# Second layer: a ring of eight activation buffers, second products held back ahead of the decays, decays a turn ahead, softplus without a mask

## What is computed

```
dt = softplus(u @ W_dt.T + b_dt)                     # u: layer-normed x, per token and channel
state = exp(dt * A[:, n]) * state + dt * B[:, n] * u # n = 0..15, along 512 tokens
y = sum_n C[:, n] * state_n + D * u
probs = softmax(u @ router_w + router_b)             # 64 experts; the best 8, renormed, are cw
routed = sum_e cw_e * (silu(u @ W1_e + b1_e) @ W2_e + b2_e)      # W1_e 128x32, W2_e 32x128
shared = sum_s silu(u @ sW1_s + sb1_s) @ sW2_s + sb2_s           # 2 experts of width 256
x = x + y + routed + shared
```

## Time and profile before

| | us |
|---|---|
| median of 3 runs | 469.74 |
| lowest and highest | 465.57, 470.54 |
| span of the profiled execution | 473.9 |
| PE busy in it | 346.5 |
| DVE busy | 347.8 |
| ACT busy | 261.5 |
| POOL busy | 243.2 |

### The profile page before, as it was taken

The page is one execution under the profiler, slowest core; times in us unless marked ns, Lnnn a source line. Parts: engine busy times, 40 slices in busy tenths (PEclk is TensorE's granted clock), DMA queues, the critical chain, the costliest instruction groups (busy, mean ns, idle before and its releaser), DMA issues.

```text
span 473.9 us, 5780 instructions
## 1 busy us (share of the span) xinstructions
PE 346.5 (73%) x1491; PEld 247.2 (52%) x1491; DVE 347.8 (73%) x615; ACT 261.5 (55%) x440; POOL 243.2 (51%) x254
## 2 busy tenths in 40 slices
PE   1846879667975987779506848977887887887883
PEld 0435659356854866668403524544554554554542
DVE  5679998897864866648169759908688688688674
ACT  1477654546458346374505675355856856856820
POOL 3475300704763676776800049005577877877850
PEclk9977675959997898998956975997999999999997
DMA  6374100100111112120160000004658658668574
GB/s 175 94 200 128 25 1 1 45 11 24 46 39 29 34 41 81 43 42 21 35 190 0 0 0 2 0 0 89 126 101 161 123 116 163 122 119 162 112 152 111
DMA packets 36213, 35.09 MB, mean 74 GB/s; under 512 B 12166, under 2 KB 30839, under 8 KB 36183
## 3 DMA queue, kind: packets, MB, share of 16 engines
q0 software_dynamic: 7104, 21.90, 22.7%
q1 hardware_dynamic: 29078, 12.84, 10.2%
HBM read 13.29 MB, written 4.65 MB: 38 GB/s over the span
## 4 chain that ended last, share of the span: by engine, by line
PE 35%; POOL 19%; DVE 19%; issue 13%; ACT 6%; DMA 3%; another core or an unknown queue 2%; DVEq 1%; SPq 0%; POOLq 0%; ACTq 0%
POOL state L568 10%; PE psum L1376 5%; POOL xn_tok L572 4%; PE psum L1349 4%; POOL g_hi L581 3%; PE psum L1365 3%; PE psum L1389 3%; PE psum L1443 3%; PE psum L292 3%; PE psum L293 2%; PE psum L294 2%; PE psum L1352 2%; PE psum L1355 2%; PE psum L1338 1%
## 5 line engine op out<-in xcount | busy, mean ns | idle before, releaser
L1212 DVE TENSOR_TENSOR_SCAN state<-dec,win_t 128x1024 f32<-128x1024 f32 x32 | 73.4, 2293 | 26.5 <-ACT dec L777 26.5
L568 POOL TENSOR_SCALAR state<-state,ssm_cb 128x1024 f32<-128x1024 f32 x32 | 49.7, 1553 | 48.0 <-DVE state L1212 45.0
L812 ACT ACTIVATE sil<-psum,vec_t 128x512 f32<-128x512 f32 x64 | 43.2, 687 | 48.3 <-PE psum L294 37.7
L509 POOL DMA_INDIRECT parts<-t_out,part x39 | 41.0, 1050 | 48.3 <-ACT t_out L726 41.9
L1498 PE MATMUL psum<-hid,g_w 128*128 128x512 f32 x128 | 62.1, 599 | 0.0
L1221 DVE TENSOR_TENSOR hid<-sil,psum 128x512 f32<-128x512 f32 x64 | 41.7, 676 | 12.9 <-ACT sil L812 10.9
L497 POOL DMA_INDIRECT x_tile<-normed,token x39 | 41.3, 1059 | 13.4 <-issue 10.7
L292 PE MATMUL psum<-xn_hi,g_hi 128*128 128x512 f32 x64 | 39.7, 620 | 11.3 <-ACT sil L812 11.3
L1094 DVE TENSOR_TENSOR t_hid<-t_sil,psum 128x352 f32<-128x352 f32 x39 | 20.3, 521 | 32.3 <-ACT t_sil L710 23.5
L717 ACT ACTIVATE t_hid_t<-psum 128x384 f32<-128x384 f32 x39 | 19.2, 492 | 38.9 <-PE psum L1365 25.3
L1376 PE MATMUL psum<-w_out,t_hid_t 128*128 x234 | 37.5, 300 | 2.2 <-ACT t_out L726 1.4
(11 more groups left out here) (308 smaller groups left out, 887.6 us busy)
## 6 DMA issues: line engine op xcount, KB each, us to landing
xn_tok<-state POOLq DMA_DIRECT2D x32, 512.0 KB, 4.5
e_raw<-in_L_ffn_w SPq DMA_DIRECT2D x16, 128.0 KB, 2.2
both<-parts SPq DMA_DIRECT2D x4, 512.0 KB, 5.6
e_raw<-in_L_ffn_w SPq DMA_DIRECT2D x8, 176.0 KB, 2.6
res<-in_L_attn_x SPq DMA_DIRECT2D x4, 256.0 KB, 3.8
normed<-rows SPq DMA_DIRECT2D x1, 1024.0 KB, 5.2
g_raw<-in_L_ffn_w SPq DMA_DIRECT2D x16, 64.0 KB, 2.3
g_w<-in_L_ffn_w SPq DMA_DIRECT2D x16, 64.0 KB, 2.2
```

The lines of the kernel that those rows point to most:

```text
L509: pool.indirect_dma_start(out=parts, out_offset=bass.IndirectOffsetOnAxis(ap=part[:, n:n + 1], axis=0), in_=t_out[n % ORING][:, :], in_off ...
L568: own(pool.tensor_scalar(state[k][:, :], state[k][:, :], ssm_cb[:, i * GPI + k // 2:i * GPI + k // 2 + 1], 0.0, ALU.mult, ALU.add))
L812: act.activation(sil[:, c % 2, :], ps[c % 2][:, :], ACT.Silu, bias=vec_t[:, V_B1 + c // NBLK:V_B1 + c // NBLK + 1]).then_inc(h_silu, 1)
L1212: dve.tensor_tensor_scan(state[k][:, :], dec[n % DECS][:, at_half], win_t[:, at_half], 0.0, ALU.mult, ALU.add).then_inc(scanned, 1)
```

## The change

- `hid` becomes a ring of eight buffers for shared and expert units alike, `sil` one of four, the decays one of six.
- PE's order is one loop over 80 units u (16 shared, 64 expert). At step u it makes the routing-weight product of unit u + 1, the input product of u + 2, and second products up to u - behind(u). `behind` is 2 as a rule, but 3, 4, 5 and 6 over the four steps ahead of a pair of decays (and of the routing's exponential, at 6), then 1: four units without a second product, then six (five at the first) in a row.
- ACT makes the decays at fixed units (14, 22, 30, 38, 46, 53, 60, 67). The first pair now stands ahead of shared SiLU 14; the pair at 22 is scanned from unit 25 on. The turns from 46 on have seven units.
- DVE's scans stand ahead of the units of `SCAN_BEFORE`: in a turn, two with two weighings behind each, then two in a row.
- The routing's exponential moves behind six shared SiLUs; Abs and Exp of softplus stand at each block's time step, the logarithms ahead of all SiLUs. The weights' copies stand together ahead of SiLU 12, and DVE's `split_cw` behind softplus.
- Softplus loses mask and select: the logarithm's bias is 1 - 3e-7 and the greater of it and a polynomial is taken. POOL's polynomial is as before. For blocks 2 and 3 ACT squares once and DVE has three instructions instead of four, a mask and a select.
- PE makes the time-step products of blocks 0 and 1 ahead of the logits' turning.
- POOL clears the decays' first columns earlier, multiplies scan 0 before it sets `y_t`, and splits a group's weights ahead of the scan that `SCAN_BEFORE` gives.

```diff
-        DECS = 3
+        HRING, SRING, DECS = 8, 4, 6
+        WEIGHTS_AT, CW_AT, COPIES_AT = 6, 11, 12
+        DECAYS_AT = {u: (2 * i, 2 * i + 1) for i, u in enumerate((14, 22, 30, 38, 46, 53, 60, 67))}
+        SCAN_BEFORE = [SHARED, SHARED, SHARED + 2, SHARED + 4]
+        for u0 in (22, 30, 38, 46, 53, 60):
+            SCAN_BEFORE += [u0 + 3, u0 + 5, u0 + 7, u0 + 7]
+        SCAN_BEFORE = [u - SHARED for u in SCAN_BEFORE + [70, 71, 73, 75]]
+        def behind(u):
+            for at_unit in (WEIGHTS_AT, *DECAYS_AT):
+                if 0 <= at_unit - 1 - u <= 4:
+                    return (1, 6, 5, 4, 3)[at_unit - 1 - u]
+            return 2
...
+            weigh_state(0)
             pool.wait_ge(cw_turned, NBLK)
             own(pool.tensor_scalar(y_t, u_t, vec_t[:, V_D:V_D + 1], 0.0, ALU.mult, ALU.add))
+            add_state(0)
+            g = GPI
+            for k in range(1, NSCAN):
+                while g < NG and (g - GPI + 1) * NBLK <= SCAN_BEFORE[k]:
+                    split_next(g)
+                    g += 1
+                weigh_state(k)
+                add_state(k)
...
+            for u in range(SHARED + UNITS):
+                if u == WEIGHTS_AT:
                     act.wait_ge(r1_arg, 1)
                     act.activation(pair[:, :, :], pair[:, :, :], ACT.Exp).then_inc(r1_exp, 1)
+                if u == min(DECAYS_AT):
+                    act.wait_ge(win_ready, NBLK)
+                for n in DECAYS_AT.get(u, ()):
+                    decay(n)
+                if u == COPIES_AT:
                     for b in range(NBLK):
                         copy_cw(b)
+                if u < SHARED:
+                    shared_silu(u)
+                else:
+                    silu(u - SHARED)
...
+            softplus(3)
+            softplus(0)
+            softplus(1)
+            for b in range(NBLK):
+                split_cw(b)
+            dve.wait_ge(firsts_ready, 1)
+            k = 0
+            for c in range(UNITS):
+                while k < NSCAN and SCAN_BEFORE[k] == c:
+                    scan(k)
+                    k += 1
+                weigh(c)
...
+            for u in range(SHARED + UNITS):
+                if u == CW_AT:
                     turn_cw(0)
                     turn_cw(1)
                     second_biases(0)
                     turn_cw(2)
                     second_biases(1)
                     turn_cw(3)
                     second_biases(2)
                     second_biases(3)
+                if SHARED <= u + 1 < SHARED + UNITS:
+                    expert_weights(u + 1 - SHARED)
+                if u + 2 < SHARED:
+                    shared_in(u + 2)
+                elif u + 2 < SHARED + UNITS:
+                    expert_in(u + 2 - SHARED)
+                while done <= u - behind(u):
+                    if done < SHARED:
+                        shared_out(done)
+                    else:
+                        expert_out(done - SHARED)
+                    done += 1
```

## The result

| | before | after |
|---|---|---|
| median, lowest to highest | 468.58 us, 465.57 to 470.54 | 476.59 us, 473.57 to 479.38 |
| ratio, 95% interval | | 1.0178, 1.0117 to 1.0238 |
| span of the profiled execution | 473.9 us | 477.6 us |
| layer norm of the second layer starts | 252.74 us | 245.04 us |

The spans differ by less than the medians because the profiled execution of the kernel before had a first layer 7.7 us longer, which the change doesn't touch. From the layer norm to the end it is 221.2 us before and 232.6 after. That is 3.4 us more than the medians differ by: one trace stands for each kernel, and in the thirteen traces of changed kernels, whose first layer is the same, the norm starts anywhere from 243.1 to 247.1 us. To hold the prediction's times against the trace of after, 7.7 us are added to the latter.

The account below looks back on a forecast made before the run. No engine was full; waits sat at the turn's seam. First turn to 331.1, then 15.8 + 16.0 + 16.9 and 16.0 + 16.5 + 16.0 to 428.3, plus 23 and 9.85: span 461.2, median 457 us, range 449 to 466.

Parts of the forecast that it names:

- PE, DVE and ACT alone: In the loop, decays hidden under six second products: 15.8 us for eight units, 14.95 for seven.
- rival (1): In the loop, POOL stays out of the way, its late products fitting between scans: 452 us; chance 0.25.
- PE, not the transfer, releases DVE: At the end, the last y transfer lands at about 450, hidden behind PE's work; that gives 2.2 us.
- the first turn of 16.7: First loop turn, 314.4 to 331.1: PE 14.3 us, 1.0 behind ACT's decays, 1.4 behind scans.
- rival (4): In the loop, held-back products delay SP's first-weight loads; with 7 us landings six turns grow by 3.8: 480 us; chance 0.05.
- The rival's point of decision: In the loop, late weight loads make the kernel slower than before from landings of about 5.8 us on.
- the split asked for ahead of C's product is caught between them: In a loop turn, POOL's weight split runs between the back-to-back third and fourth scans, done at 14.8 us.
- POOL's whole price: In the loop, POOL's lateness brings turns of 16 to 16.9 us: span 461.2 us, against 456.3 with POOL out of the way.
- Rival (2): POOL loses the race at 2.25 against 2.29, its split 3.7 us late: turns of 18.2 and 17.5, 462 us; chance 0.14.
- 16.0, 16.5 and 16.0 for those of seven: The loop's last three turns, seven units each, 14.95 us without blocking, lengthened by POOL's late products and splits.
- The prediction's own sign of being wrong: In the loop, splits holding PE for over 2 us a turn would show the forecast wrong.
- the front: Ahead of the loop, first weighing at 316.8 instead of 322.5: gain 5.7 us, with 4 us pause and lower clock at turnings.

Follow-up runs that it names:

- e2_load_early: The changed kernel with SP loading a group's first weights once those two groups before are split, second weights one group later: 469.52 us, 1.0035 of the kernel before.
- e6_load_no_product: The changed kernel with first weights loaded early and POOL's product with C times B left out: 453.1 us, 0.9685 of the kernel before.
- e7_load_spread: The changed kernel with early loads, scans ahead of units 2, 4, 6 and 7, and at most five second products held back: 462.8 us, 0.990 of the kernel before.
- e1_apart: The changed kernel with the fourth scan of each middle turn one unit after the third instead of right behind it: 481.0 us, 1.030 of the kernel before.

## Why the prediction was wrong

It said 457 us, faster with 0.86, and had 449 to 466 as its range. Its steps, one by one:

**Right: PE, DVE and ACT alone.** 15.8 and 14.95 us a turn were 15.86 and 14.94 once POOL and the loads were out of the way, and that kernel took 453.1 us, where rival (1) said 452. At the end PE, not the transfer, releases DVE (2.69 us of idle, for the earlier trace rows's 4.76). The first shared SiLU at 276.7 (277.0 with the 7.7 us added), the routing Exp done at 285.9 (285.9), the weights at 291.7 (291.3) and the first turn of 16.7 (16.9) held.

**Wrong, 7.1 us: the loads.** This was rival (4), given 0.05. Its chain, from the held-back products through SP to POOL, was as put there; two steps failed. One is the landing time, "2.3 us" from the median of the earlier trace rows, and the argument that this median includes the loop: of the three loads that POOL waited for two landed in 5.43 and 4.50 us. The other is that I asked only whether the split came in time for PE. The first of the three landed in 2.20 us, as assumed, and POOL stood 4.49 us for it with its products queued behind the split, where the prediction's own 16.1 of 17.7 us leave it 1.6 to spare in a turn; turns 2 and 3 are 16.1 and 18.1 us where early loads make them 15.9 and 16.8. The rival's point of decision, "about 5.8 us", doesn't come out of its figures either: 15.9 - 11.4 - 1.3 leaves 3.2 us for a landing, and the 12.7 us between 461.2 and 473.9 are 2.1 more in each of six turns, so 5.3. It cost a full 7 us in three places rather than a little in six.

**Wrong, some 11 us: POOL.** The sum had "the split asked for ahead of C's product is caught between them", done at 14.8, and turns of 16 to 16.9; POOL's whole price was 461.2 - 456.3 = 4.9 us. Measured: 16.4 us (`e2_load_early` against `e6_load_no_product`), with the split done at about 18 us and turns of 18.06. One step that failed is the serving order. I serialised the reads, yet let POOL's product in between two scans in a row. B's product, issued 0.74 us into C, was done only behind D (4.56 us), and everything behind it on POOL slid by 2.3 us, one scan. Rival (2), 0.14, gave 18.2 for such a turn, which is what came, through another product than the one it named.

That is the smaller part: 18.1 for 16.9 in turn 4. The step that cost more is "16.0, 16.5 and 16.0 for those of seven": with early loads turns 6 and 7 are 18.4 and 22.7, 8.6 of the 11 us. The sum had a split late by 1.1 us at most. PE waits 2.41 us for one in turn 6 and 5.18 in turn 7, where the split's parts run beside C and D, and behind both waits its products take 0.63 us instead of 0.39. The sum had no slow clock in the loop at all. The prediction's own sign of being wrong, splits that hold PE for over 2 us, came in the last four such waits of after: 2.42, 2.73, 5.18 and 2.82 us. Spacing the scans (`e7_load_spread`) mends the turns of eight and not this: its turn 6 has a wait of 5.2 us. What the right place of these splits alone is worth, no run shows.

The Trainium skill (SBUF — State Buffer, "Who interferes with whom") says the first to issue holds the port. The trace agrees for each single pair: 3.10 us for a product issued 0.1 us into a scan of 2.28, 3.42 for a scan issued under a product. What my sum turned on is one step further: POOL waits, and DVE has a second scan ready. There each product was done 0.84 us behind the second scan: 4.56 us in three turns running and 5.20 in the fourth. But the first part of a split, at 428.05 in the fence above, issued 0.72 us into C, was done at 429.71, 0.1 us behind C's end (427.33 + 2.28) and long before D's at 431.84. So a short POOL instruction does get in between; and 0.84 is less than the product's 1.12, so part of a product may have too. No view shows what goes on inside an instruction.

**Wrong, 2.7 us: the front.** Gain from the layer norm to the first weighing: 3.0 us (69.8 to 66.8), not 5.7. I had seen the 4 us pause at the turnings and the lower clock behind it, but charged the clock too little: four bias products 3.78 us against 2.35, the shared inputs 0.63 against 0.39 each. And I had taken the pause as given. It was an order of DVE's that moving the calls of `split_cw` mends, worth 7.6 to 8.0 us, the largest gain of one edit.

457.0 + 7.1 + 11.5 + 2.7 is 478.3, against 476.6 measured: what was off is accounted for to 2 us, though POOL's and the loads' terms overlap where POOL waits anyway.

## What to carry to other kernels

When work is held back to cover a seam, list every semaphore that the held work raises: here the last product of a group was what a load two queues away waited for, and the cover was given back in full until the load was asked for earlier. Where two engines share a port, two long instructions back to back on one can be one long instruction to the other; space them, but look first at what the pair itself was covering. Lay every turn of both kernels side by side before explaining one: here the turn that looked typical was nearly as long as before, and the loss stood in the last two. And a pause on PE costs itself and the slow stretch behind it, so before it is accepted in a sum, see whether the engine waited for could do that piece first.

## What the runs showed of the hardware that I had not expected

- With two scans back to back on DVE, a POOL product (1.12 us alone) issued 0.7 us into the first was done 0.84 us behind the second, after 4.56 us; the first part of a split (0.29 alone), issued at the same place, was done 0.1 us behind the first, after 1.66. A weighing, with one input from SBUF and one from PSUM, lets POOL through: with one between two scans a product was 3.10 (`e1_apart`).
- Every load of 64 KB in the loop of after ran beside a 512 KB accumulating transfer. The eight issued 3.1 to 4.0 us behind one landed in 2.0 to 2.3 us, the four issued 0.4 to 2.2 us behind one, with an earlier one still under way, in 4.1 to 5.4.
- After a pause of 3.96 us PE's granted clock was 0.58 in the 10 us around it and 0.74 in the next 10, and a 128x512 product took 0.63 instead of 0.39; without the pause it stayed at 1.00. Behind the waits of 2.42 and 5.18 us in the loop of after products took 0.63 too.
